# Attention with three blocks of Q and K projections, scores as two 64-row chains, and two moved elementwise steps

## What is computed

```
x2 = _ln(x, ln1_g, ln1_b)
q, k, v = split(x2 @ in_proj_w.T + in_proj_b)          # 12 heads of 16
scores = einsum('bqhd,bkhd->bhqk', q, k) / 4
ao = einsum('bhqk,bkhd->bqhd', softmax(scores), v)
x = x + ao @ out_proj_w.T + out_proj_b
xm = _ln(x, ln2_g, ln2_b)
probs = softmax(xm @ router_w.T + router_b); topw, topi = top_k(probs, 2)
out = sum over e of combine[:, e] * (gelu(xm @ w1[e] + b1[e]) @ w2[e] + b2[e])
return x + out
```

## Time and profile before

| | us |
|---|---|
| median of 3 runs | 1377.45 (1376.71 to 1379.24) |
| the profiled execution | 1375.09 |
| its span, first to last instruction | 1373.3 |
| attention, from the first scores to the first turned expert rows | 805.97 to 1054.83 |
| from there to the end | 318.5 |
| mean granted TensorE clock | 0.942 |

### The profile page before, as it was taken

One profiled execution on the slowest core, in us unless ns is written; L12 is line 12 of the kernel. 1 busy time (PEld: TensorE's weight loads), 2 busy tenths in 40 slices (PEclk: granted clock), 3 DMA queues, 4 the chain that ended last, 5 costly groups with the idle time before them and its releaser, 6 DMA issues.

```text
span 1373.3 us, 19692 instructions
## 1 busy us (share of the span) xinstructions
PE 1213.5 (88%) x5844; PEld 785.5 (57%) x5845; DVE 1006.6 (73%) x2119; ACT 694.5 (51%) x1478; POOL 742.4 (54%) x469
## 2 busy tenths in 40 slices
PE   7986875669898999999887799999999899999996
PEld 5432442325454554545443568888888677777774
DVE  5998797988999999898999536778888553333332
ACT  1346333676777868686855245545553232222221
POOL 3148642886969696978778300135555564222222
PEclk9987877789999999999999899999999799999998
DMA  6200012240413213040410001112222233222221
GB/s 184 59 1 0 28 38 98 91 148 12 136 48 102 89 59 127 20 147 0 147 33 1 1 30 42 56 53 59 58 69 75 47 55 47 37 36 36 36 36 21
DMA packets 72833, 81.09 MB, mean 59 GB/s; under 512 B 13314, under 2 KB 64865, under 8 KB 72753
## 3 DMA queue, kind: packets, MB, share of 16 engines
q1 hardware_dynamic: 53418, 69.20, 16.0%
q0 software_dynamic: 17152, 9.24, 5.0%
q10 hardware_dynamic: 2184, 1.72, 0.5%
HBM read 48.77 MB, written 30.01 MB: 57 GB/s over the span
## 4 chain that ended last, share of the span: by engine, by line
PE 61%; DVE 18%; ACT 11%; issue 6%; POOL 2%; DMA 1%; DVEq 0%; SPq 0%; ACTq 0%; POOLq 0%
PE ps L2263 10%; PE ps L1047 7%; PE ps L2282 7%; DVE hs L1330 4%; PE ps L1647 4%; PE ps L1019 3%; PE ps L1705 3%; PE ps L952 3%; ACT ps L1195 3%; PE ps L1720 2%; PE ps L275 2%; PE ps L2272 2%; PE ps L268 2%; PE ps L994 2%; DVE ps L205 2%
## 5 line engine op out<-in xcount | busy, mean ns | idle before, releaser
L1447 POOL TENSOR_TENSOR Bx<-dtz,Bb 128x984 f32<-128x984 f32 x128 | 287.8, 2270 | 47.5 <-DVE hs L1330 34.2
L1330 DVE TENSOR_TENSOR_SCAN hs<-ps,Bx 128x492 f32<-128x492 f32 x256 | 287.5, 1164 | 15.9 <-POOL Bx L1447 12.2
L1047 PE MATMUL ps<-hs,b_id 128*128 128x492 f32 x512 | 236.9, 586 | 8.5 <-ACT y L1213 7.2
L1195 ACT ACTIVATE ps<-dt,A 128x324 f32<-128x324 f32 (+1 forms) x512 | 210.5, 456 | 56.2 <-DVE hs L1330 53.6
L2382 POOL DMA_INDIRECT out<-yt,dest x48 | 74.7, 1556 | 171.4 <-DVE yt L2368 158.8
L1340 DVE TENSOR_TENSOR hs<-hs,ps 128x984 f32<-128x984 f32 x128 | 150.3, 1174 | 2.9 <-issue 0.7
L2263 PE MATMUL ps<-W,xT 97*128 (+1 forms) x384 | 144.1, 519 | 3.5 <-issue 2.4
L1047 PEld LDWEIGHTS ps<-hs,b_id 128*128 128x128 f32 x512 | 93.3, 195 | 75.3 <-issue 69.6
L2352 DVE COPY hT__6145<-ps 128x768 f32<-128x768 f32 x48 | 45.9, 957 | 112.4 <-PE ps L2272 111.0
L2320 ACT ACTIVATE hb<-ps 128x768 f32<-128x768 f32 x48 | 38.9, 810 | 144.2 <-PE ps L2263 138.0
L2282 PE MATMUL ps<-W,hT__6145 128*128 x576 | 109.2, 327 | 0.8 <-DVE yb L2362 0.8
(11 more groups left out here) (281 smaller groups left out, 2399.2 us busy)
## 6 DMA issues: line engine op xcount, KB each, us to landing
Bb<-b_rows SPq DMA_DIRECT2D x32, 656.0 KB, 6.8
buckets<-b_zero SPq DMA_DIRECT2D x8, 2288.0 KB, 15.2
xg<-buckets SPq DMA_DIRECT2D x48, 104.0 KB
xc<-in_xcol SPq DMA_DIRECT2D x4, 1176.0 KB, 9.5
W<-in_w1d SPq DMA_DIRECT2D x8, 582.0 KB
W<-in_w2d SPq DMA_DIRECT2D x8, 576.0 KB
out<-H SPq DMA_DIRECT2D x8, 246.0 KB
H<-P SPq DMA_DIRECT2D x8, 147.0 KB
```

Source lines behind the costliest of these rows:

```text
L1047: mm = pe.matmul(ps[:, BANK_Y + h, 0:HALF], ident[:], f2(hs[:, s % LONG])[:, h * HALF:(h + 1) * HALF], start=s == 0, stop=s == STATE - 1)
L1195: a = act.activation(ps[:, BANK_A + h, c:c + w].rearrange("p (g t) -> p g t", t=S)[:, :, 1:S], dt[:, (par + t // STATE) % 2, m, g0 * S:g1 ...
L1330: v.tensor_tensor_scan(f2(hs[:, t % LONG])[:, c], ps[:, BANK_A + h, 0:HALF], f2(Bx[:, t % RING])[:, c], 0.0, ALU.mult, ALU.add).then_inc(s ...
L1447: g.tensor_tensor(Bx[:, t % RING], dtz[:, p], Bb[:, p, t % STATE, :].rearrange("p (a n) -> p a n", a=1).broadcast_to([128, NI, N]), ALU.mu ...
```

## The change

It changes four things in attention.

- **Three blocks instead of six.** Block 0 holds the Q of heads 0 to 7, packed 16 rows a head. Block 1 holds their K. Block 2 (`_shared`) holds Q and K of heads 8 to 11, in runs of 32 rows. ScalarE copies the K block 4 times over all 128 rows, each time with a per-row scale (`V_KM`) and bias that are zero outside the head's rows, and block 2 with 6 activations over 32 rows (`keep_others`). A round has 11 of these activations where it had 15, and 6 matmuls where it had 12. The memset of `kB` shrinks, and one of `qT` comes in.
- **Scores as two chains.** The four matmuls of a sequence now contract over 64 rows each, two over rows 0 to 63 into one PSUM bank, two over rows 64 to 127 into the other, in the order low, high, low, high, with 164, 328, 328 and 164 columns. `HEAD_AT` says where each head then lies.
- **`normed` moves from VectorE to GpSimd**, behind the root that it needs and ahead of the sum into `H`. TensorE turns these rows behind the heads instead of ahead of them.
- **ScalarE copies all turned probabilities** in one activation of 984 columns; VectorE's copy of 492 columns is gone, and `s_PT` takes the place of the two semaphores.

The diff, cut to its core:

```
@@ @@ def attention_front
-    kB = sb("kB", [128, 2, 3, G, 4, S]); V = ...
-    qT = sb("qT", [128, 2, 3, N])
+    kB = sb("kB", [128, 2, 12 * N]); V = ...
+    qT = sb("qT", [128, 2, 2, N])
+    kB0 = [kB[:, par, 0:4 * N].rearrange("p (g h s) -> p g h s", g=G, h=4) for par in range(2)]
+    kB1 = [kB[:, par, 4 * N:6 * N].rearrange("p (g h s) -> p g h s", g=G, h=2) for par in range(2)]
...
-        g.memset(kB[:], 0.0).then_inc(s_cst, 1)
+        g.memset(kB[:, :, 4 * N:6 * N], 0.0).then_inc(s_cst, 1)
+        g.memset(qT[:, :, 1, :], 0.0).then_inc(s_cst, 1)
...
-        for m_ in range(3):
-            act.wait_ge(s_q, j * 3 + (m_ + 1))
-            act.activation(qT[:, par, m_, :], ps[:, place(f"Q{m_}"), 0:N], ACT.Identity, bias=qb[:, m_:m_ + 1],
-                           scale=0.25).then_inc(s_qT, 1)
+        act.wait_ge(s_q, j + 1)
+        act.activation(qT[:, par, 0, :], ps[:, place("Q0"), 0:N], ACT.Identity, bias=qb[:, 0:1], scale=0.25).then_inc(s_qT, 1)
...
         for h in range(4):
-            c = slice(32 * h, 32 * h + 32)
-            a = act.activation(kB[c, par, m_, :, h, :], ps[c, place(f"K{m_}"), 0:N].rearrange("p (g s) -> p g s", g=G),
-                               ACT.Identity, bias=vec[c, V_KB + m_:V_KB + m_ + 1])
+            a = act.activation(kB0[par][:, :, h, :], ps[:, place("K0"), 0:N].rearrange("p (g s) -> p g s", g=G),
+                               ACT.Identity, bias=vec[:, V_KB + h:V_KB + h + 1], scale=vec[:, V_KM + h:V_KM + h + 1])
+        a.then_inc(s_kT, 1)
+
+    def keep_others(act, j, par, place):
+        act.wait_ge(s_k, j * 2 + 2)
+        for first in (0, 64):
+            q, k = slice(first, first + 32), slice(first + 32, first + 64)
+            act.activation(qT[q, par, 1, :], ps[q, place("QK"), 0:N], ACT.Identity, bias=qb[q, 1:2], scale=0.25)
+            for h in range(2):
+                a = act.activation(kB1[par][q, :, h, :], ps[k, place("QK"), 0:N].rearrange("p (g s) -> p g s", g=G),
+                                   ACT.Identity, bias=vec[k, V_K2B + h:V_K2B + h + 1], scale=vec[k, V_K2M + h:V_K2M + h + 1])
         a.then_inc(s_kT, 1)
@@ @@ ending, TensorE
                 fr.project(pe, "Q0", 0, fr.s_q)
-                fr.project(pe, "Q1", 1, fr.s_q)
-                fr.project(pe, "Q2", 2, fr.s_q)
-                fr.project(pe, "K0", 3, fr.s_k)
+                fr.project(pe, "K0", 1, fr.s_k)
+                fr.project(pe, "QK", 2, fr.s_k)
                 post(last, 1, 12, None)
                 post(last, 1, 13, None)
-                pe.wait_ge(fr.s_qT, 2)
-                fr.project(pe, "K1", 4, fr.s_k)
-                fr.project(pe, "K2", 5, fr.s_k)
@@ @@ attention, TensorE
-                    for h0, h1 in ((0, 4), (4, 6), (6, 8), (8, 12)):
-                        m_, j = h0 // 4, h0 % 4
-                        mm = pe.matmul(ps[0:S, SCORES + h0 // 6, (h0 % 6) * S:(h0 % 6 + h1 - h0) * S],
-                                       qT[:, par, m_, q * S:(q + 1) * S], kB[:, par, m_, q, j:j + h1 - h0, :].rearrange("p h s -> p (h s)"),
-                                       start=True, stop=True)
+                    for a, keys, m_, h0, h1 in ((0, kB1, 1, 4, 6), (1, kB0, 0, 0, 4), (0, kB0, 0, 0, 4), (1, kB1, 1, 4, 6)):
+                        half = slice(64 * a, 64 * a + 64)
+                        mm = pe.matmul(ps[0:S, SCORES + a, h0 * S:h1 * S], qT[half, par, m_, q * S:(q + 1) * S],
+                                       keys[par][half, q].rearrange("p h s -> p (h s)"), start=True, stop=True)
                     mm.then_inc(s_s, 1)
-                if q == 1 and is_round(i - 2):
-                    normed_rows(i)
...
                     mm.then_inc(s_av, 1)
+                if q == 1 and is_round(i - 2):
+                    normed_rows(i)
@@ @@ attention, ScalarE
-                    act.activation(flat(PT[:, c % 2, 0:6, :]), ps[0:S, FLIP, 0:6 * S], ACT.Copy).then_inc(s_PTa, 1)
+                    act.activation(PT[:, c % 2].rearrange("p (a h) s -> p a (h s)", a=2), ps[0:S, FLIP:FLIP + 2, 0:6 * S], ACT.Copy).then_inc(s_PT, 1)
@@ @@ attention, VectorE
-                    v.tensor_copy(flat(PT[:, c % 2, 6:12, :]), ps[0:S, FLIP + 1, 0:6 * S]).then_inc(s_PTv, 1)
...
-                if q == 0 and is_round(i - 2):
-                    normed(i - 2, par)
@@ @@ attention, GpSimd
+            def normed(p, par):
+
+                g.wait_ge(s_rr, p + 1)
+                if p in (ROUNDS - 3, ROUNDS - 1):
+                    g.wait_ge(s_pad, 1 if p == ROUNDS - 3 else 2)
+                elif is_round(p - 2):
+                    g.wait_ge(s_sc, min(p - 1, FULL_ROUNDS) * (16 * 2 * G))
+                xs_ = slots(p)
+                for c in range(G):
+                    g.tensor_scalar(xs_[:, c, 0:D], XN[:, par, c, :], mg[:, c, 0:1], rr[:, c:c + 1], ALU.subtract, ALU.mult)
+                g.tensor_copy(xs_[:, :, D + EXPERTS:D + EXPERTS + 1],
+                              token[:, bass.ds(p * G, G)].rearrange("p (b a) -> p b a", a=1)).then_inc(s_xn, 1)
...
+                    normed(p, par)
```

More of the change, by code:

```diff
@@ L77 @@
 V_QB = 114
-V_KB = 117
-V_ROW = 120
-V_H_NORM = 121
-V_HF_NORM = 123
-V_N = 125
+V_KM = 116
+V_KB = 120
+V_K2M = 124
+V_K2B = 126
+V_ROW = 128
+V_H_NORM = 129
+V_HF_NORM = 131
+V_N = 133
 CH = 4
@@ L1630, in free @@
                     _, off, s_free, per, at = SIDE_TILES[k]
+                    if s_free is None:
+                        continue
                     r = i + off if k >= 0 else i - 1 + off
@@ L1655, in front @@
                     pe.wait_ge(s_x2T, j * 2 + 2)
-                    for m_ in range(3):
-                        project(f"Q{m_}", m_, s_q, j)
-                    project("K0", 3, s_k, j)
+                    project("Q0", 0, s_q, j)
+                    project("K0", 1, s_k, j)
                 if q == 2:
-                    project("K1", 4, s_k, j)
-                    project("K2", 5, s_k, j)
+                    project("QK", 2, s_k, j)
                 if q == 3:
@@ L1718, in step @@
                     at_least(pe, s_x3, i * G + (q - 3))
-                    for h in range(HEADS):
-                        mm = pe.matmul(ps[0:S, HEAD_OUT + c % 2, h * (DH + 1):(h + 1) * (DH + 1)], PT[:, c % 2, h, :], V[:, vpar, c, h, :],
+                    for n, h in enumerate(HEAD_AT):
+                        mm = pe.matmul(ps[0:S, HEAD_OUT + c % 2, h * (DH + 1):(h + 1) * (DH + 1)], PT[:, c % 2, n, :], V[:, vpar, c, h, :],
                                        start=True, stop=True)
                     mm.then_inc(s_av, 1)
+                if q == 1 and is_round(i - 2):
+                    normed_rows(i)
                 if behind(i, q, 3):
@@ L1788, in front @@
                     fr.keep_queries(act, j, par, bank)
-                for m_ in {1: (0,), 2: (1, 2)}.get(q, ()):
-                    fr.keep_keys(act, j, par, m_, bank)
+                    fr.keep_keys(act, j, par, bank)
+                if q == 2:
+                    fr.keep_others(act, j, par, bank)
             def route(i, par, q):
@@ L1934, in col @@
                 return a.rearrange("p (b a) -> p b a", a=1).broadcast_to(W)
-            def normed(p, par):
-                v.wait_ge(s_rr, p + 1)
-                if p in (ROUNDS - 3, ROUNDS - 1):
-                    v.wait_ge(s_pad, 1 if p == ROUNDS - 3 else 2)
-                elif is_round(p - 2):
-                    v.wait_ge(s_sc, min(p - 1, FULL_ROUNDS) * (16 * 2 * G))
-                xs_ = slots(p)
-                for c in range(G):
-                    v.tensor_scalar(xs_[:, c, 0:D], XN[:, par, c, :], mg[:, c, 0:1], rr[:, c:c + 1], ALU.subtract, ALU.mult)
-                v.tensor_copy(xs_[:, :, D + EXPERTS:D + EXPERTS + 1],
-                              token[:, bass.ds(p * G, G)].rearrange("p (b a) -> p b a", a=1)).then_inc(s_xn, 1)
             def pick(p):
@@ L2088, in _ @@
             t.step(0, 0)
-            normed(ROUNDS - 1, 1 - par)
             hb = H[:, (ROUNDS - 1) * G:B, :]
@@ L2133, in norm @@
                     g.tensor_tensor(rr[:], ms[:], nh[:, 0:G], ALU.pow).then_inc(s_rr, 1)
+                    if p == ROUNDS - 3:
+                        g.wait_ge(s_k, ROUNDS * 2)
+                        g.memset(XS_more[0][:], 0.0).then_inc(s_pad, 1)
+                    normed(p, par)
                     if p < ROUNDS - 1:
@@ L2435, in _haar, with _shared, _only @@
     return np.where(odd % 2 == 1, -0.0625, 0.0625).astype(np.float32)
-def _heads(a):
+def _shared(q, k):
     import numpy as np
-    a = np.asarray(a).reshape(12, 16, -1)
-    out = np.zeros((12, 32, a.shape[2]), a.dtype)
-    out[:, 0:16] = a
-    return out.reshape(384, -1)
+    return np.concatenate([q[128:160], k[128:160], q[160:192], k[160:192]])
+def _only(a, size, number):
+    import numpy as np
+    p = np.arange(128)
+    return np.stack([np.where(p % (size * number) // size == n, a, 0) for n in range(number)], axis=1).astype(np.float32)
 def _layout(x):
```

67 lines of the change are left out of this document (29 added, 38 removed).

## The result

The change took 1386.66 us (median of 10 runs, 1382.3 to 1419.2), beside 1375.68 us for the kernel before on the same chips. The ratio is 1.009, with a 95% interval of 1.0065 to 1.0114. Its profiled execution took 1386.09 us at a span of 1384.3, with 1375.09 before. The forecast was 1371.8, with a range of 1363 to 1379.5. Two of the 10 runs, of 1418 and 1419 us, count as slow and are left out of the ratio; the other eight still spread over 18 us, where before spreads over 6.

What follows compares the result with a forecast made beforehand. TensorE bounds attention and would save 40 us, but wait 35 us for xg behind the SyncE queue; experts start 5.7 us earlier, so 1375.09 becomes 1369.4, plus 2.4 for the median: 1371.8, range 1363 to 1379.5.

Steps and rivals of the forecast that it cites:

- What bounds attention: In attention, TensorE was taken as the bound, busy for 248 of 255 us.
- The SyncE queue as the next bound: Behind attention, the queue of loads would land xg only at 1050.1, with TensorE there near 1015.
- Projections and scores: In attention's rounds, TensorE would lose 25.1 us of projections and 23 us of scores.
- My rule of lengths: In the scores, 0.143 us per 164-column pass, 64-row chains overlapping: 7 lengths instead of 12, 1.00 us a sequence.
- Waits on ScalarE: In attention, TensorE would wait 10 us in all for head outputs copied behind K activations, ends 0 and 20.
- GpSimd: In attention, its new 192-column tensor_scalar would take 0.9 us, between 0.59 and 1.05; busy time 119 us, far from 200.
- End of the Mamba layer: Where the Mamba layer ends, fewer projections would save 1.8 us, bounds 1.2 and 3.5, and start the SyncE queue earlier.
- From the turn to the experts: From turning xg to the first expert matmul, 7.65 us instead of 8.61, as the wait for XN goes.
- The 0.8 us in the forecast for a start at half clock: After TensorE's wait for xg, half clock would add 0.6 us to the turn and 0.2 to the heads.
- wait of 35 us: Ahead of the turn of xg, TensorE would stand idle for 35 us until the rows land at 1050.1.
- the sum for TensorE: Up to the turn of xg, -25.1 - 23 + 10 - 1.8 = -40 us, ends -5 and -52, arriving near 1015.
- slower, through the clock at the restart: Rival: behind the wait for xg, half-clock stretches cost up to 7.4 us each, two giving 1386; chance 0.12.

Runs made afterwards that it cites:

- e4: The change with its four score matmuls over all 128 rows instead of 64, heads' scores summed in pairs; 1376.99 us, ratio 0.998.
- e8: The change with three projections kept but scores over 128 rows, all results computed through zero-padded key slots; 1375.43 us, ratio 0.9991.
- e11: The change with the four 64-row score matmuls of each sequence computed twice; 1377.53 us, ratio 0.9994.
- e1: The kernel before with only the other engines' parts: ScalarE's full copy, normed rows on GpSimd, heads ahead of their turn; 1373.79 us, ratio 0.9967.
- e9: The change with 128-row scores, all results computed, and each W1 load split into 96 partitions and one; 1344.53 us, ratio 0.977.
- e14: The kernel before with only the moved copy, normed rows on GpSimd and new order, plus W1 loads split; 1370.46 us, ratio 0.9957.
- e10: The change with its 64-row score matmuls reordered, both of one chain and then both of the other; 1382.69 us, ratio 1.0031.
- e5: The change with each W1 load split into its first 96 partitions and its last one; 1383.16 us over four widely spread runs.
- e3: The change with each Q and K projection of the loop computed twice; 1389.78 us, ratio 1.0087.
- e12: The change with the 17-column head matmuls of each sequence computed twice; 1564.95 us, ratio 1.1363.
- e13: The change with the score chains of one sequence in four computed five times, the others once; 1398.03 us, ratio 1.0181.
- e2: The change with only TensorE's parts left: VectorE copies half the turned probabilities and writes normed rows, old order; 1401.92 us, ratio 1.0162.
- e6: The kernel before with each W1 load split into its first 96 partitions and its last one; 1376.75 us, ratio 1.0012.

## Why the prediction was wrong, point by point

- **What bounds attention:** right, TensorE. It is what made the clock matter in full.
- **The SyncE queue as the next bound:** right as a mechanism, but the change never got that far. It shows where the clock is better: waits for `xg` of 17.72 us in e4, 8.10 in e8, 4.94 in e11, 2.9 in e1, at turns between 1056.7 and 1059.2 (forecast: 1050.1), and it is gone in e9 and e14, with the split. The times of e4, e8 and e11, 1375 to 1378, are 4 to 6 us above my 1371.8: `xg` was issued at 1050 to 1054 there and not near 1045, since the last W2 left at 998 to 1002 instead of 996, and `out` took 43 to 45 us of issuing as before.
- **Projections and scores:** the scores took 0.99 us in the view of the chain, which is the one that the forecast of 1.00 was read from (1.06 in the timeline, beside before's 1.83). The whole work taken away was 44.6 us at full clock, for 48.1 forecast (25.1 and 23). My rule of lengths behind the 1.00 isn't shown, though: by it e10 would have taken 1.6 us, and it took 1.07.
- **Waits on ScalarE:** 10 us forecast; TensorE's waits on it and on VectorE in attention are two of 0.5 and 0.8 us, beside one of 1.8 at the start that before has too (2.0). **GpSimd:** 0.9 us forecast for a `tensor_scalar`, inside bounds of 0.59 and 1.05, 1005 ns measured:

```profile
L2124 POOL TENSOR_SCALAR XS<-XN,c_mg,c_rr 82x192 f32<-82x192 f32 x24 | 24.0, 1005 | 1.5 <-DMA buckets<-XS,c_slot 0.9 <-POOL XS L2134 0.2
```

- **End of the Mamba layer:** 1.8 us forecast and measured. **From the turn to the experts:** 7.65 us forecast, behind a wait; 7.34 measured without one, at a clock that was at half already (0.50 from 1069.79 to 1077.13). The 0.8 us in the forecast for a start at half clock behind a wait stand in no row of before, and no run has a wait of 35 us. What the runs showed is about 0.7: behind waits of 2.92 us (e1), 4.94 (e11), 8.10 (e8) and 17.72 (e4) the turn took 1.06 to 1.16 us, where it took 0.60 before, the heads 3.45, where they took 3.20, and the way to the experts 7.35 to 7.45. In the change and in e5 the turn took 1.06 us without a wait too. The experts, taken as unchanged, came out 2.7 us shorter.
- **The step that failed** is the sum for TensorE, -40 us, "It arrives at the turn of `xg` near 1015". All its terms were durations at full clock, and I took it for granted that TensorE would keep that clock: the sum has no term for it. The clock took 60.7 us more than before, so TensorE came at 1069.79, and the wait of 35 us that the forecast rests on never came about. The row was there: at 907.36 before, the clock fell to half for 6.84 us, just behind scores, the turn of `XS` and heads, during the turning of the probabilities, with no idle time in the view. Two lines of before's windows, on either side of it:

```profile
901.00:907.00 6.00, 5.93 (x63) 5.05 (x61) 5.62 (x19) 3.64 (x6) 0.59 (x1) 1.00 0.08 28
907.36:914.20 6.84, 6.84 (x24) 5.13 (x23) 4.66 (x19) 2.06 (x4) 2.15 (x2) 0.50 0.06 26
```

I had read the clock only behind the seam, and so placed the risk at a restart after idling. The rival "slower, through the clock at the restart" has the right cause and by chance the right number, 1386, but the wrong place and mechanism: there was no idling and no restart. Its 0.12 was too low, because I didn't ask what the removed matmuls had done for the clock.

The longest fall in the change has no wait in the view either: TensorE was busy for 44.3 of 44.3 us at a clock of 0.50 (907.3 to 951.6).

**What stays open:** which property of the stream lets the clock fall. From the 0.75 of the change, more wide matmul work brought it to 0.90 over 64 rows (e11), to 0.91 with scores over 128 (e4) and to 0.86 with projections (e3), added narrow matmuls brought it to 0.58 (e12), and the work of e11 in one place to 0.85 (e13). The runs don't tell why. The profile models when a matmul ends, so pauses inside a busy stretch might not show in it. Open too are the 10 to 15 us between e2 and the change, the 4 to 8 between e10 and the change, and e9's clock above e8's.

## What to carry to other kernels

Before you take wide matmuls out of a stage that TensorE bounds, look for places where its granted clock already falls without an idle gap, and ask whether the work that is left is mostly narrow. If so, price the rest at half clock too, keep the wide work spread among the narrow (a clock of 0.90 in e11, 0.85 in e13), and don't take all of it: here the saving in the projections alone paid (e9, 0.977), and that in the scores as well didn't (the change, 1.009). And when a stage gets shorter, free the queue behind it in the same step, since neither the split (e6: 1.0012) nor the lighter TensorE work (e8: 0.9991) gained anything alone, and together they gave 0.977. The larger part of that last gain is clock, and that the split brings it isn't shown.

## What the runs showed of the hardware that I had not expected

- The clock halves under a TensorE for which the profile shows no idle time: 0.50 from 907 to 951 us in the change, 0.58 as a mean over 255 us in e12. Computing the 17-column matmuls twice, 62 us at full clock by the reckoning, cost 178 us.
- More work can take less time: e4 has 0.8 us more of scores in each of 32 sequences than the change and is about 10 us faster.
- The four 64-row matmuls of a sequence take 1.07 us when each half's two are issued in a row (e10) and 1.06 us interleaved, against 1.82 us over 128 rows (e4): the order makes no difference.
- With each W1 load of 97 partitions issued as 96 and 1, the queue has issued the loads of all eight experts in 32 us instead of 195 (802.6 to 834.6 in e9, at 227 GB/s), and `out`, from 866 on, waits only for its data.
